# Attention scores and softmax of two 128-token blocks handled as one piece

## The chip, the cores and the metric

The kernel runs on one core of a Trainium2 chip. The metric is the device time of one launch in microseconds (us). Five engines work side by side and meet through semaphores: TensorE (PE in the profile, with its weight loads as PEld), VectorE (DVE), ScalarE (ACT), GpSimd (POOL) and SyncE (SP, which here only issues DMAs).

## What is computed

One transformer layer over x of 32 x 256 tokens x 256 features, in fp32: cross-attention with 8 heads to a context of 77 tokens, then a feed-forward network (FFN) with ternary weights, each behind a layer norm and with a residual.

```python
q = _heads(x @ Wq.T + bq)                 # x: layer norm of the input
k = _heads(y @ Wk.T + bk)                 # y: the 77 context tokens
v = _heads(y @ Wv.T + bv)
logits = einsum('bhqd,bhkd->bhqk', q, k) * scale + causal
attn = softmax(logits, axis=-1)
out = einsum('bhqk,bhkd->bhqd', attn, v) ... @ Wo.T + bo
# FFN: D_IN 256, D_HID 1024
h = silu(_tlin(x, w1_w, w1_s)) * _tlin(x, w2_w, w2_s)
h = gelu(_tlin(h, h1_w, h1_s)); h = gelu(_tlin(h, h2_w, h2_s))
return _tlin(h, w3_w, w3_s)
```

The causal mask is laid over 256 queries and 77 keys, so of a sequence's two blocks of 128 queries only the first has masked scores.

## The kernel before

The 8192 tokens are cut into 16 tiles of 512 tokens: two sequences (NB = 2), or four blocks of 128 tokens (NQ = 4, TQ // P = 2 of each sequence). The program is a software pipeline of passes. A first pass (the list FIRST, for `f is None`) does the attention of tile 0 while the weights arrive, are rounded (ROUND, on ACT) and compared (CHECK, on DVE). Then 15 passes do the FFN of tile f and the attention of tile f + 1 together, and a 16th does only the FFN of the last tile. 14 of the 15 are turns of a loop, the other two passes are written out behind it.

What stands next to what is an order written out by hand: the list ORDER of pairs (step, n). Every engine runs through the same list and issues, at each entry, whatever that step has for it; between engines there are only semaphores. So an entry's place in ORDER is its place in each engine's queue, and an instruction that waits holds up all that stands behind it on its engine.

The steps that matter here:

- L1 0 to 7 (FFN, first layer): PE 8 matmuls of 512 columns in two products (gate and up), ACT Silu of the gate (L492) and the rounding `a_hi` of the entry before (L501), DVE the product with up (L602) and the remainder `a_lo` of the entry before (L607). L1E does the last remainder. The `a_lo` feed L2.
- L2 0 to 7: PE 16 matmuls each; ACT two Gelu activations (L506, L507, the second signals `gelu2_done`); DVE the remainder `b_lo` (L613). L2 0 waits for `h1_done` before each of its k.
- S 0 to 3, one for each block of 128 tokens: 8 small matmuls (L434, each two instructions in the trace, so 16) write the scores of 8 heads to columns 0 to 153 of the four banks `att_banks`. Blocks 0 and 2 are masked straight from the banks by DVE (L637, signals `masked`), blocks 1 and 3 copied by ACT (L526, signals `s_copied`); since all four blocks use the same columns, PE waits for the read of the one before. DVE then takes the maximum per head (L641) and subtracts it (L643, signals `shifted`).
- EXP 0 to 3: ACT the exponential (L530, waits `shifted`), DVE in `soften` the sum (L578, waits `exp_done`), its reciprocal (L580) and the scaling (L582, signals `probs_ready`).
- PT 0 to 3: PE 8 transposes of the probabilities (L445), copied out half by ACT (L535) and half by DVE (L650, signals `pt_dve_done`). PV 0 and 1 (L454) multiply with v for one sequence and wait until both copies of both its blocks are done.

ACT holds one table of functions at a time. Silu, Gelu and Exp are in different ones, and the compiler puts an ACT_TABLE_LOAD ahead of the first activation that needs another.

Of the kernel before, what the change touches and what calls it, by code (L numbers as in the profile page):

```python
# [19 lines left out]
ALU = mybir.AluOpType  # L20
ACT = mybir.ActivationFunctionType
AX_X = mybir.AxisListType.X

P = 128
B, TQ, TK, D = 32, 256, 77, 256
H = 8
HD = D // H
HID = 1024
TILE = 512
NB = TILE // TQ  # L30
NT = B // NB
NQ = TILE // P
KD = D // P
KH = HID // P
HG = H // 4
G2 = 2 * TK


def column_of(head):
# [3 lines left out]
SCALE = float(HD) ** -0.5  # L43
# [6 lines left out]

ORDER = [
    ("L1", 0), ("T1", 0), ("L1", 1), ("KV", 0), ("L1", 2), ("Q", 0), ("L1", 3), ("S", 0),
    ("L1", 4), ("L1", 5), ("S", 1), ("L1", 6), ("S", 2), ("L1", 7), ("L1E", 0), ("S", 3),
    ("EXP", 0), ("EXP", 1), ("EXP", 2), ("EXP", 3),
# [10 lines left out]
def steps(ffn, att, nxt):  # L65
# [5 lines left out]

FIRST = [
    ("KV", 0), ("T1", 0), ("ROUND", 0), ("ROUND", 1), ("Q", 0), ("CHECK", 0), ("CHECK", 1), ("ROUND", 2),
    ("S", 0), ("S", 1), ("S", 2), ("ROUND", 3), ("S", 3), ("CHECK", 2), ("EXP", 0), ("EXP", 1), ("ROUND", 4), ("EXP", 2),
    ("EXP", 3), ("PT", 0), ("CHECK", 3), ("PT", 1), ("ROUND", 5), ("CHECK", 4), ("PV", 0),
    ("PT", 2), ("ROUND", 6), ("CHECK", 5), ("PT", 3), ("CHECK", 6), ("PV", 1), ("ROUND", 7), ("CHECK", 7), ("O", 0),
    ("ROUND", 8), ("CHECK", 8), ("ROUND", 9), ("CHECK", 9), ("ROUND", 10), ("CHECK", 10), ("COUNT", 0),
    ("LN2S", 0), ("LN2A", 0), ("T2", 0), ("LN1S", 0), ("LN1A", 0), ("CTX", 0),
]
# [2 lines left out]
def build_kernel(nc, x, ctx_t, w_att, vectors, w1, w2, h1, h2, w3, out):  # L82
# [4 lines left out]
    with ExitStack() as es:  # L87
# [36 lines left out]
        q_t, _ = put("q_t", [P, HG, TILE], at=b_lo_at + 4096)  # L124
# [16 lines left out]
        k_t, _ = put("k_t", [P, HG, NB * TK])  # L141
# [3 lines left out]
        probs, probs_at = put("probs", [P, NQ, H * TK])  # L145
# [4 lines left out]
        mask, _ = put("mask", [P, TK])  # L150
# [5 lines left out]
        mx, _ = put("mx", [P, NQ, H])  # L156
        total, _ = put("total", [P, NQ, H])
        rtotal, _ = put("rtotal", [P, NQ, H])
# [14 lines left out]
        ab = es.enter_context(nc.psum_tensor("att_banks", [P, 4, 512], F32))  # L173
# [22 lines left out]
        masked, s_ready, max_done, shifted, exp_done = sem("masked"), sem("s_ready"), sem("max_done"), sem("shifted"), sem("exp_done")  # L196
        s_copied = sem("s_copied")
        sum_done, rsum_done, probs_ready = sem("sum_done"), sem("rsum_done"), sem("probs_ready")
        pt_ready, pt_act_done, pt_dve_done = sem("pt_ready"), sem("pt_act_done"), sem("pt_dve_done")
        pv_ready, heads_done, o_ready = sem("pv_ready"), sem("heads_done"), sem("o_ready")  # L200
        x_biased, x1_done, x1_kept = sem("x_biased"), sem("x1_done"), sem("x1_kept")
# [30 lines left out]
        at = 0  # L232
# [68 lines left out]
        def _(pe):  # L301
# [37 lines left out]
            def one_pass(f, a, nxt, general):  # L339
                for step, n in steps(True, a is not None, nxt) if f is not None else FIRST:  # L340
# [35 lines left out]
                    if step == "L4":  # L376
# [3 lines left out]
                        for i in range(2):  # L380
                            j = 2 * n + i
# [6 lines left out]
                            else:  # L388
                                mm = product(fb[:, 2 + n, i * D:(i + 1) * D], lambda k: w3_sb[:, k, :], KH, hi, lo,
                                             wait_h, KH * f, w_is_moving=True)  # L390
# [4 lines left out]
                    if step == "T1":  # L395
                        pe.wait_ge(ln_ready[0], a + 1)
                        for k in range(KD):
                            for j in range(NQ):
                                mm = nc.tensor.transpose(ab[:, k, j * P:(j + 1) * P], xln[:, j, k * P:(k + 1) * P], id32[:])  # L399
# [13 lines left out]
                    if step == "Q":  # L413
                        pe.wait_ge(ln1t_done, a + 1)
                        for m in range(HG):
                            for k in range(KD):
                                mm = nc.tensor.matmul(ab[:, m, :], wq_sb[:, k, m * P:(m + 1) * P], ln1_t[:, k, :],  # L417
                                                      start=(k == 0), stop=(k == KD - 1))
                        mm.then_inc(q_ready, 1)
                    if step == "S":  # L420
                        if n == 0:
                            pe.wait_ge(q_done, a + 1)
                            pe.wait_ge(k_done, a + 1)
                            pe.wait_ge(v_done, a + 1)
                        if n == 1 or n == 3:
                            pe.wait_ge(masked, NB * a + n // 2 + 1)
                        if n == 2:
                            pe.wait_ge(s_copied, NB * a + 1)
                        keys = (n // (TQ // P)) * TK
                        for g in range(HG):  # L430
                            at = g * TK
                            for h in range(4):
                                rows = slice(HD * h, HD * (h + 1))
                                mm = nc.tensor.matmul(ab[:, h, at:at + TK], q_t[rows, g, n * P:(n + 1) * P],  # L434
                                                      k_t[rows, g, keys:keys + TK], start=True, stop=True)
                        mm.then_inc(s_ready, 1)
                    if step == "PT":
                        pe.wait_ge(probs_ready, NQ * a + n + 1)
                        if n < 2:
                            pe.wait_ge(shifted, NQ * a + NQ)  # L440
                        if n == 3:
                            pe.wait_ge(heads_done, NB * a + 1)
                        pair = (2, 0, 0, 2)[n]
                        for h in range(H):
                            mm = nc.tensor.transpose(ab[0:TK, pair + h // 4, (h % 4) * P:(h % 4 + 1) * P],  # L445
                                                     probs[:, n, column_of(h) * TK:(column_of(h) + 1) * TK], id32[:])
                        mm.then_inc(pt_ready, 1)
# [36 lines left out]
        def _(act):  # L484
            def one_pass(f, a, nxt):
                for step, n in steps(True, a is not None, nxt) if f is not None else FIRST:
# [30 lines left out]
                    if step == "Q":  # L517
# [1 line left out]
                        for g in range(HG):  # L519
                            op = nc.scalar.activation(q_t[:, g, :], ab[:, g, :], ACT.Identity, bias=bq_sb[:, g:g + 1])  # L520
                        op.then_inc(q_done, 1)
                    if step == "S" and n % (TQ // P) == 1:
                        act.wait_ge(s_ready, NQ * a + n + 1)
                        if n == 3 and not (isinstance(a, int) and a == 0):
                            act.wait_ge(x1_kept, a)
                        nc.scalar.copy(probs[:, n, :].rearrange("p (h g c) -> p h g c", g=HG, h=4),  # L526
                                       ab[:, :, 0:G2].rearrange("p h (g c) -> p h g c", g=HG)).then_inc(s_copied, 1)
                    if step == "EXP":
                        act.wait_ge(shifted, NQ * a + n + 1)
                        nc.scalar.activation(probs[:, n, :], probs[:, n, :], ACT.Exp, scale=SCALE).then_inc(exp_done, 1)  # L530
                    if step == "PT":
                        act.wait_ge(pt_ready, NQ * a + n + 1)
                        q0 = (n % 2) * P
# [21 lines left out]
        def _(dve):  # L555
# [15 lines left out]
                                                 ALU.subtract, ALU.mult)  # L571
                op.then_inc(ln_ready[i], 1)

            def soften(n, a):

                p = probs[:, n, :].rearrange("p (h c) -> p h c", h=H)
                dve.wait_ge(exp_done, NQ * a + n + 1)
                nc.vector.tensor_reduce(total[:, n, :], p, AX_X, ALU.add).then_inc(sum_done, 1)  # L578
                dve.wait_ge(sum_done, NQ * a + n + 1)
                nc.vector.reciprocal(rtotal[:, n, :], total[:, n, :]).then_inc(rsum_done, 1)  # L580
                dve.wait_ge(rsum_done, NQ * a + n + 1)
                nc.vector.tensor_tensor(p, p, rtotal[:, n, :].unsqueeze(2).broadcast_to([P, H, TK]), ALU.mult)\  # L582
                    .then_inc(probs_ready, 1)

            def one_pass(f, a, nxt):
                for step, n in steps(True, a is not None, nxt) if f is not None else FIRST:
# [34 lines left out]
                    if step == "KV":  # L621
                        dve.wait_ge(v_ready, a + 1)
                        nc.vector.tensor_tensor(v_sb[:], ab[0:TK, 3, :].rearrange("p (b d) -> p b d", b=NB),
                                                bv_sb[0:TK].unsqueeze(1).broadcast_to([TK, NB, D]), ALU.add).then_inc(v_done, 1)
                    if step == "S":
                        scores = ab[:, :, 0:G2].rearrange("p h (g c) -> p h g c", g=HG)
                        if n % (TQ // P) == 0:
                            dve.wait_ge(s_ready, NQ * a + n + 1)
                        else:
                            dve.wait_ge(s_copied, NB * a + n // 2 + 1)  # L630
                        m = mx[:, n, :].rearrange("p (h g) -> p h g", g=HG)
                        p = probs[:, n, :].rearrange("p (h g c) -> p h g c", g=HG, h=4)
                        if n == 2 and not (isinstance(a, int) and a == 0):
                            dve.wait_ge(x1_kept, a)
                        if n % (TQ // P) == 0:

                            nc.vector.tensor_tensor(p, scores, mask[:].unsqueeze(1).unsqueeze(1).broadcast_to([P, 4, HG, TK]),  # L637
                                                    ALU.add).then_inc(masked, 1)
                            dve.wait_ge(masked, NB * a + n // 2 + 1)
                        scores = p  # L640
                        nc.vector.tensor_reduce(m, scores, AX_X, ALU.max).then_inc(max_done, 1)  # L641
                        dve.wait_ge(max_done, NQ * a + n + 1)
                        nc.vector.tensor_tensor(p, scores, m.unsqueeze(3).broadcast_to([P, 4, HG, TK]), ALU.subtract)\  # L643
                            .then_inc(shifted, 1)
                    if step == "EXP":
                        soften(n, a)
                    if step == "PT" and f is not None:
                        dve.wait_ge(pt_ready, NQ * a + n + 1)
                        q0 = (n % 2) * P
# [122 lines left out]
```

## Time and profile before

| | us |
|---|---|
| median of 3 runs | 1685.14 (1684.5 to 1686.07) |
| the profiled execution | 1688.33 |
| its span in the trace | 1686.5 |
| one pass (two stretches of 101.30 and 101.45) | about 101.4 |

The span is what the trace shows from first to last instruction; the execution's own time is 1.8 us more. Start times in the rows are us from the span's start. A timeline row is: start, duration, engine, line, operation, output and inputs, count, and in brackets the idle time of the engine ahead of it and what ended it. Matmuls overlap, so for PE the distance between two starts counts and not the duration.

### The profile page before, as it was taken

How to read it: one execution, taken by the hardware profiler on the slowest of the kernel's cores; microseconds unless marked ns; L12 is line 12 of the kernel's file. 1: busy time of each engine (PE TensorE's matmuls, PEld its weight loads, DVE VectorE, ACT ScalarE, POOL GpSimd, SP SyncE). 2: the span in 40 equal slices, each digit the busy share in tenths (PEclk: the TensorE clock that was granted, in tenths of full speed). 3: DMA queues.
4: the chain of work that ended last, by engine and by line, in shares of the span. 5: the costliest groups of instructions: out<-in, count | busy, mean ns of one | idle time of the engine just before them, and what ended most of it. 6: DMA issues, size and time to landing. Idle time of an engine off the chain costs nothing.

```text
span 1686.5 us, 22398 instructions
## 1 busy us (share of the span) xinstructions
PE 1636.5 (97%) x9090; PEld 1324.1 (79%) x9090; DVE 818.4 (49%) x1449; ACT 742.9 (44%) x1136; POOL 119.1 (7%) x120
## 2 busy tenths in 40 slices
PE   4599999999999999999999999999999999999998
PEld 3478888787887878888787887878888787887887
DVE  6663634637255463634637255462644636345331
ACT  5453543535344353543535345353443535345342
POOL 1100101001010100101001010100101001010000
PEclk7699999999999999999999999999999999999999
DMA  7100000000000000000000000000000000000000
GB/s 300 42 1 13 16 12 16 0 16 12 12 16 0 21 7 12 16 9 19 0 16 12 12 16 0 16 12 12 16 1 27 0 16 12 12 17 1 1 13 13
DMA packets 21094, 32.60 MB, mean 19 GB/s; under 512 B 976, under 2 KB 19408, under 8 KB 19536
## 3 DMA queue, kind: packets, MB, share of 16 engines
q1 hardware_dynamic: 21072, 32.30, 5.6%
q8 instruction: 15, 0.25, 0.1%
q14 instruction: 7, 0.06, 0.0%
HBM read 23.91 MB, written 8.39 MB: 19 GB/s over the span
## 4 chain that ended last, share of the span: by engine, by line
PE 86%; DVE 8%; issue 3%; ACT 2%; DMA 0%; POOL 0%; DVEq 0%; SPq 0%; POOLq 0%; ACTq 0%
PE ffn_banks L309 68%; PE att_banks L445 4%; PE att_banks L462 3%; PE att_banks L417 3%; PE att_banks L454 2%; DVE a_lo L607 2%; DVE a_f L602 2%; PE att_banks L410 2%; DVE mx L641 2%; DVE probs L637 1%; PE att_banks L405 1%; PE att_banks L399 1%; PE att_banks L336 1%; DVE stage L595 1%; PE att_banks L434 1%
## 5 line engine op out<-in xcount | busy, mean ns | idle before, releaser
L309 PE MATMUL ffn_banks<-a_hi,h_sb 128*128 128x512 f32 x1024 | 408.6, 399 | 0.0
L309 PE MATMUL ffn_banks<-b_hi,h_sb 128*128 128x512 f32 x1024 | 401.3, 392 | 0.0
L309 PE MATMUL ffn_banks<-a_lo,h_sb 128*128 128x512 f32 x1024 | 400.2, 391 | 0.0
L309 PE MATMUL ffn_banks<-b_lo,h_sb 128*128 128x512 f32 x1024 | 398.6, 389 | 0.0
L506 ACT ACTIVATE a_f<-ffn_banks,vec 128x512 f32<-128x512 f32 x128 | 88.2, 689 | 354.2 <-PE ffn_banks L309 354.2
L613 DVE TENSOR_TENSOR a_lo<-a_f,a_hi 128x512 fp32r<-128x512 f32 x128 | 88.6, 692 | 317.8 <-ACT a_hi L507 317.8
L309 PEld LDWEIGHTS ffn_banks<-a_hi,h_sb 128*128 128x128 f32 x1024 | 192.3, 188 | 46.0 <-issue 6.2
L613 DVE TENSOR_TENSOR b_lo<-b_f,b_hi 128x512 fp32r<-128x512 f32 x128 | 85.8, 690 | 286.1 <-ACT b_hi L507 286.1
L309 PEld LDWEIGHTS ffn_banks<-b_hi,h_sb 128*128 128x128 f32 x1024 | 192.3, 188 | 39.8
L309 PEld LDWEIGHTS ffn_banks<-b_lo,h_sb 128*128 128x128 f32 x1024 | 192.3, 188 | 39.7
L309 PEld LDWEIGHTS ffn_banks<-a_lo,h_sb 128*128 128x128 f32 x1024 | 192.5, 188 | 38.4
L309 PE MATMUL ffn_banks<-ln_hi,w_sb 128*128 128x512 f32 x512 | 217.5, 425 | 2.4 <-DVE ln_lo L667 2.4
L309 PE MATMUL ffn_banks<-ln_lo,w_sb 128*128 128x512 f32 x512 | 202.5, 396 | 0.0
L506 ACT ACTIVATE b_f<-ffn_banks,vec 128x512 f32<-128x512 f32 x128 | 88.0, 688 | 249.2 <-PE ffn_banks L309 249.0
L492 ACT ACTIVATE a_f<-ffn_banks,vec 128x512 f32<-128x512 f32 x128 | 88.2, 689 | 178.3 <-PE ffn_banks L309 178.3
L602 DVE SCALAR_TENSOR_TENSOR a_f<-ffn_banks,vec,a_f 128x512 f32<-128x512 f32 x128 | 95.7, 748 | 145.4 <-ACT a_f L492 104.1
L309 PE MATMUL ffn_banks<-w_sb,a_hi 128*128 128x256 f32 x512 | 124.9, 286 | 0.4 <-DVE a_lo L613 0.4
L309 PE MATMUL ffn_banks<-w_sb,a_lo 128*128 128x256 f32 x512 | 123.5, 283 | 0.0
L309 PEld LDWEIGHTS ffn_banks<-ln_hi,w_sb 128*128 128x128 f32 x512 | 97.1, 190 | 28.6 <-issue 3.6
L309 PEld LDWEIGHTS ffn_banks<-ln_lo,w_sb 128*128 128x128 f32 x512 | 97.3, 190 | 21.8 <-issue 3.6
L692 POOL TENSOR_TENSOR veps<-mv,eps 128x4 f32<-128x4 f32 x32 | 6.4, 201 | 1336.6 <-DVE mv L564 1336.6
L309 PEld LDWEIGHTS ffn_banks<-w_sb,a_hi 128*128 128x128 f32 x512 | 98.2, 192 | 0.7 <-DVE a_lo L613 0.6
(81 smaller groups left out, 1942.6 us busy)
## 6 DMA issues: line engine op xcount, KB each, us to landing
x_in<-in_x SPq DMA_DIRECT2D x16, 512.0 KB, 3.8
stage<-in_h SPq DMA_DIRECT2D x8, 1024.0 KB, 14.2
out<-out_sb SPq DMA_DIRECT2D x16, 512.0 KB, 2.9
stage<-in_w SPq DMA_DIRECT2D x3, 1024.0 KB, 9.2
ctx_sb<-in_ctx_t SPq DMA_DIRECT2D x16, 154.0 KB, 2.2
w_att_sb<-in_w_att SPq DMA_DIRECT2D x1, 1024.0 KB, 7.2
vec<-in_vectors SPq DMA_DIRECT2D x1, 402.0 KB, 4.5
```

The costliest lines, as they stand in the source:

```text
L309: mm = nc.tensor.matmul(psum, left, right, start=(k == 0 and part == 0), stop=(k == rows - 1 and part == 1))
L410: mm = nc.tensor.matmul(ab[0:TK, 3, b * D:(b + 1) * D], ctx_sb[:, k, b * TK:(b + 1) * TK], wv_sb[:, k, :], start=(k == 0), stop=(k == KD - 1))
L417: mm = nc.tensor.matmul(ab[:, m, :], wq_sb[:, k, m * P:(m + 1) * P], ln1_t[:, k, :], start=(k == 0), stop=(k == KD - 1))
L445: mm = nc.tensor.transpose(ab[0:TK, pair + h // 4, (h % 4) * P:(h % 4 + 1) * P], probs[:, n, column_of(h) * TK:(column_of(h) + 1) * TK], i ...
L454: mm = nc.tensor.matmul(ab[HD * h:HD * (h + 1), bank, g * TQ:(g + 1) * TQ], v_sb[:, n, (4 * g + h) * HD:(4 * g + h + 1) * HD], attn_t[:, 4 ...
L462: mm = nc.tensor.matmul(ab[:, 2 + j // 2, (j % 2) * D:(j % 2 + 1) * D], heads_t[:, k, j * P:(j + 1) * P], wo_sb[:, k, :], start=(k == 0), ...
L492: nc.scalar.activation(a_f32[:, n, :], fb[:, 2 * (n % 2), :], ACT.Silu, scale=s1_sb[:, n:n + 1]).then_inc(silu_done, 1)
L506: nc.scalar.activation(f32[:, n, :], fb[:, n % 4, :], ACT.Gelu, scale=scale[:, n:n + 1])
L602: nc.vector.scalar_tensor_tensor(out=a_f32[:, n, :], in0=fb[:, 2 * (n % 2) + 1, :], scalar=s2_sb[:, n:n + 1], in1=a_f32[:, n, :], op0=ALU. ...
L607: nc.vector.tensor_tensor(a_lo[:, m, :], a_f32[:, m, :], a_hi[:, m, :].bitcast(F32), ALU.subtract)\
L613: nc.vector.tensor_tensor(lo[:, n, :], f32[:, n, :], hi[:, n, :].bitcast(F32), ALU.subtract).then_inc(done, 1)
L641: nc.vector.tensor_reduce(m, scores, AX_X, ALU.max).then_inc(max_done, 1)
```

## The change

S now has two entries, one for each sequence. Each issues 16 matmuls: those of the first block to columns 0 to 153 of each bank, those of the second to columns 154 to 307. ACT copies both blocks (1232 elements per partition) to `probs`, and DVE works from there only. What DVE did under S and EXP is split into steps of their own: MASK n (first block only, 616 elements), MAX n and SUB n and SOFT n (both blocks, 1232 elements, 16 sums). EXP n is one activation over 1232 elements. PT 0 waits for `probs_ready` of sequence 0 and for `s_copied` of sequence 1, PT 2 for `probs_ready` of sequence 1. In ORDER, SOFT 0 stands ahead of L2 0, MAX 1 and SUB 1 behind it, EXP 1 behind L2 1, and SOFT 1 between PT 0 and L2 3. FIRST is changed in the same manner.

```diff
 ORDER = [
     ("L1", 0), ("T1", 0), ("L1", 1), ("KV", 0), ("L1", 2), ("Q", 0), ("L1", 3), ("S", 0),
-    ("L1", 4), ("L1", 5), ("S", 1), ("L1", 6), ("S", 2), ("L1", 7), ("L1E", 0), ("S", 3),
-    ("EXP", 0), ("EXP", 1), ("EXP", 2), ("EXP", 3),
-    ("L2", 0), ("L2", 1), ("L2", 2), ("PT", 0), ("L2", 3), ("PT", 1), ("L2", 4), ("PV", 0),
+    ("L1", 4), ("MASK", 0), ("L1", 5), ("MAX", 0), ("S", 1), ("L1", 6), ("SUB", 0), ("L1", 7), ("L1E", 0),
+    ("EXP", 0), ("MASK", 1), ("SOFT", 0), ("L2", 0), ("MAX", 1), ("SUB", 1), ("L2", 1), ("EXP", 1),
+    ("L2", 2), ("PT", 0), ("SOFT", 1), ("L2", 3), ("PT", 1), ("L2", 4), ("PV", 0),
...
-                        if n == 1 or n == 3:
-                            pe.wait_ge(masked, NB * a + n // 2 + 1)
-                        if n == 2:
+                        else:
                             pe.wait_ge(s_copied, NB * a + 1)
...
+                        for half in range(2):
+                            tokens = slice((2 * n + half) * P, (2 * n + half + 1) * P)
+                            for g in range(HG):
+                                at = half * G2 + g * TK
+                                for h in range(4):
+                                    rows = slice(HD * h, HD * (h + 1))
+                                    mm = nc.tensor.matmul(ab[:, h, at:at + TK], q_t[rows, g, tokens],
+                                                          k_t[rows, g, n * TK:(n + 1) * TK], start=True, stop=True)
                         mm.then_inc(s_ready, 1)
                     if step == "PT":
-                        pe.wait_ge(probs_ready, NQ * a + n + 1)
-                        if n < 2:
-                            pe.wait_ge(shifted, NQ * a + NQ)
+                        if n % 2 == 0:
+                            pe.wait_ge(probs_ready, NB * a + n // 2 + 1)
+                        if n == 0:
+                            pe.wait_ge(s_copied, NB * a + NB)
...
-                        act.wait_ge(shifted, NQ * a + n + 1)
-                        nc.scalar.activation(probs[:, n, :], probs[:, n, :], ACT.Exp, scale=SCALE).then_inc(exp_done, 1)
+                        act.wait_ge(shifted, NB * a + n + 1)
+                        nc.scalar.activation(probs[:, 2 * n:2 * n + 2, :], probs[:, 2 * n:2 * n + 2, :],
+                                             ACT.Exp, scale=SCALE).then_inc(exp_done, 1)
...
+                    if step == "MASK":
+                        dve.wait_ge(s_copied, NB * a + n + 1)
...
+                    if step == "MAX":
+                        dve.wait_ge(masked, NB * a + n + 1)
+                        nc.vector.tensor_reduce(per_head(mx, n), heads_of(n), AX_X, ALU.max).then_inc(max_done, 1)
+                    if step == "SUB":
+                        dve.wait_ge(max_done, NB * a + n + 1)
+                        nc.vector.tensor_tensor(heads_of(n), heads_of(n), over_keys(mx, n), ALU.subtract).then_inc(shifted, 1)
+                    if step == "SOFT":
+                        dve.wait_ge(exp_done, NB * a + n + 1)
+                        nc.vector.tensor_reduce(per_head(total, n), heads_of(n), AX_X, ALU.add).then_inc(sum_done, 1)
+                        dve.wait_ge(sum_done, NB * a + n + 1)
+                        nc.vector.reciprocal(per_head(rtotal, n), per_head(total, n)).then_inc(rsum_done, 1)
+                        dve.wait_ge(rsum_done, NB * a + n + 1)
+                        nc.vector.tensor_tensor(heads_of(n), heads_of(n), over_keys(rtotal, n), ALU.mult).then_inc(probs_ready, 1)
```

ACT's queue from the last remainder's rounding of L1 on (`a_hi`), before; `b_f` and `b_hi` are the two Gelu of an L2 entry, `attn_t` the copy of PT 0:

```order
L501 CAST a_hi<-a_f_58 128x512 x2
L523 REGISTER_ALU
L526 COPY probs<-att_banks 128x616
L529 REGISTER_ALU
L530 ACT_TABLE_LOAD
L530 ACTIVATE probs<-probs 128x616 x2
L529 REGISTER_ALU
L530 ACTIVATE probs<-probs 128x616 x2
L506 ACT_TABLE_LOAD
L506 ACTIVATE b_f_59<-ffn_banks,vec 128x512
L507 ACTIVATE b_hi<-ffn_banks,vec 128x512
```

And now:

```order
L502 CAST a_hi<-a_f_58 128x512 x2
L531 ACT_TABLE_LOAD
L531 ACTIVATE probs<-probs 128x1232
L507 ACT_TABLE_LOAD
L507 ACTIVATE b_f_59<-ffn_banks,vec 128x512
L508 ACTIVATE b_hi<-ffn_banks,vec 128x512
L507 ACTIVATE b_f_59<-ffn_banks,vec 128x512
L508 ACTIVATE b_hi<-ffn_banks,vec 128x512
L531 ACT_TABLE_LOAD
L531 ACTIVATE probs<-probs 128x1232
L507 ACT_TABLE_LOAD
L507 ACTIVATE b_f_59<-ffn_banks,vec 128x512
```

The four exponentials stood together, between one pair of table loads. Now there are two, with the Gelu of L2 0 and L2 1 between them, and a pair of table loads for each.

DVE's queue from L2's first remainder (`b_lo`) to the copy of PT 1 (`attn_t`), before:

```order
L582 TENSOR_TENSOR probs<-probs,rtotal 128x616
L613 TENSOR_TENSOR b_lo<-b_f_59,b_hi 128x512 x3
L650 COPY attn_t<-att_banks 77x4x128
L613 TENSOR_TENSOR b_lo<-b_f_59,b_hi 128x512
L650 COPY attn_t<-att_banks 77x4x128
```

And now:

```order
L645 TENSOR_TENSOR probs<-probs,rtotal 128x1232
L616 TENSOR_TENSOR b_lo<-b_f_59,b_hi 128x512
L635 TENSOR_REDUCE mx<-probs 128x16
L638 TENSOR_TENSOR probs<-probs,mx 128x1232
L616 TENSOR_TENSOR b_lo<-b_f_59,b_hi 128x512 x2
L647 ISA
L649 COPY attn_t<-att_banks 77x4x128
L641 TENSOR_REDUCE total<-probs 128x16
L643 RECIPROCAL rtotal<-total 128x16
L645 TENSOR_TENSOR probs<-probs,rtotal 128x1232
L616 TENSOR_TENSOR b_lo<-b_f_59,b_hi 128x512
L647 REGISTER_ALU
```

Maximum and subtraction of sequence 1 moved behind the first `b_lo`, and its sum, reciprocal and scaling stand between the copy of PT 0 and that of PT 1, which is the next row.

## Rows read from the trace of the kernel before

**Rows 1.** The page: busy time, share of the span, instructions of PE

```profile
PE 1636.5 (97%) x9090; PEld 1324.1 (79%) x9090; DVE 818.4 (49%) x1449; ACT 742.9 (44%) x1136; POOL 119.1 (7%) x120
```

**Rows 2.** Busy time of each engine in one pass; the 1.00 is PEclk

```profile
184.30:285.75 101.45, 101.35 (x571) 82.09 (x570) 49.80 (x89) 45.00 (x71) 7.38 (x7) 1.00 0.04 12
```

**Rows 3.** Timeline of PE in that pass, from S 0 to PV 0

```profile
194.13 0.68 PE L434 MATMUL att_banks<-k_t,q_t 32*128 32x77 f32 x16
194.74 0.50 PE L309 MATMUL ffn_banks<-ln_hi,w_sb 128*128 128x512 f32 x1
...
199.25 0.50 PE L309 MATMUL ffn_banks<-ln_hi,w_sb 128*128 128x512 f32 x1
...
201.93 0.50 PE L309 MATMUL ffn_banks<-ln_hi,w_sb 128*128 128x512 f32 x1
...
224.96 1.07 PE L454 MATMUL att_banks<-attn_t,v_sb 77*32 77x256 f32 x16
```

**Rows 4.** The same timeline cut off at 194.20: only S 0's first instructions

```profile
194.13 0.35 PE L434 MATMUL att_banks<-k_t,q_t 32*128 32x77 f32 x4
```

**Rows 5.** Timeline of PE's weight loads: those of S 0 and of S 3

```profile
194.12 0.54 PEld L434 LDWEIGHTS att_banks<-k_t,q_t 32*128 32x128 f32 x16 [0.36 <-issue]
...
204.15 0.54 PEld L434 LDWEIGHTS att_banks<-k_t,q_t 32*128 32x128 f32 x16 [0.53 <-DVE probs L637]
```

**Rows 6.** Timeline of DVE, L1 6 to L1 7

```profile
202.04 0.74 DVE L602 SCALAR_TENSOR_TENSOR a_f<-ffn_banks,vec,a_f 128x512 f32<-128x512 f32 x1
202.70 0.68 DVE L607 TENSOR_TENSOR a_lo<-a_f,a_hi 128x512 fp32r<-128x512 f32 x1
203.30 0.79 DVE L637 TENSOR_TENSOR probs<-att_banks,mask 128x616 f32<-128x616 f32 x1
...
204.96 0.80 DVE L643 TENSOR_TENSOR probs<-probs,mx 128x616 f32<-128x616 f32 x1
205.68 0.74 DVE L602 SCALAR_TENSOR_TENSOR a_f<-ffn_banks,vec,a_f 128x512 f32<-128x512 f32 x1
```

**Rows 7.** Timeline of DVE, softmax of block 0, and the copy of PT 0

```profile
209.71 0.80 DVE L578 TENSOR_REDUCE total<-probs 128x8 f32<-128x616 f32 x1 [0.37 <-ACT probs L530]
210.54 0.20 DVE L580 RECIPROCAL rtotal<-total 128x8 f32<-128x8 f32 x1
210.78 0.80 DVE L582 TENSOR_TENSOR probs<-probs,rtotal 128x616 f32<-128x616 f32 x1
...
218.63 0.68 DVE L650 COPY attn_t<-att_banks 77x512 f32<-77x512 f32 x1
```

**Rows 8.** Timeline of ACT, from the last `a_hi` to the first Gelu

```profile
206.45 0.62 ACT L501 CAST a_hi<-a_f 128x512 fp32r<-128x512 f32 x1 [2.10 <-DVE a_f L602]
...
208.96 2.55 ACT L530 ACTIVATE probs<-probs 128x616 f32<-128x616 f32 x4
211.52 1.28 ACT L506 ACT_TABLE_LOAD   x1
212.82 0.69 ACT L506 ACTIVATE b_f<-ffn_banks,vec 128x512 f32<-128x512 f32 x1
213.40 0.68 ACT L507 ACTIVATE b_hi<-ffn_banks,vec 128x512 fp32r<-128x512 f32 x1
```

**Rows 9.** Groups of instructions: line, engine, form, count, busy us, mean ns

```profile
L530 ACT ACTIVATE probs<-probs 128x616 f32<-128x616 f32 x64 | 40.8, 707 | 0.2
L510 ACT COPY ln_t<-att_banks 128x1024 f32<-128x1024 f32 x16 | 16.1, 1004 | 5.5 <-PE att_banks L399 5.5
L658 DVE TENSOR_TENSOR x<-att_banks,x_in 128x1024 f32<-128x1024 f32 x16 | 19.6, 1225 | 23.4 <-PE att_banks L462 23.4
```

**Rows 10.** Timeline of ACT at the pass's start: Silu's table and its first user

```profile
173.43 1.28 ACT L492 ACT_TABLE_LOAD   x1
180.72 0.69 ACT L492 ACTIVATE a_f<-ffn_banks,vec 128x512 f32<-128x512 f32 x1 [6.01 <-PE ffn_banks L309]
```

**Rows 11.** Timeline of PE in the first pass: PV 0

```profile
40.29 1.93 PE L454 MATMUL att_banks<-attn_t,v_sb 77*32 77x256 f32 x16 [1.25 <-ACT attn_t L538]
```

More of the change, by code:

```diff
@@ L73 @@
     ("KV", 0), ("T1", 0), ("ROUND", 0), ("ROUND", 1), ("Q", 0), ("CHECK", 0), ("CHECK", 1), ("ROUND", 2),
-    ("S", 0), ("S", 1), ("S", 2), ("ROUND", 3), ("S", 3), ("CHECK", 2), ("EXP", 0), ("EXP", 1), ("ROUND", 4), ("EXP", 2),
-    ("EXP", 3), ("PT", 0), ("CHECK", 3), ("PT", 1), ("ROUND", 5), ("CHECK", 4), ("PV", 0),
-    ("PT", 2), ("ROUND", 6), ("CHECK", 5), ("PT", 3), ("CHECK", 6), ("PV", 1), ("ROUND", 7), ("CHECK", 7), ("O", 0),
+    ("S", 0), ("MASK", 0), ("MAX", 0), ("S", 1), ("SUB", 0), ("EXP", 0), ("MASK", 1), ("MAX", 1), ("SOFT", 0),
+    ("SUB", 1), ("ROUND", 3), ("EXP", 1), ("PT", 0), ("CHECK", 2), ("ROUND", 4), ("PT", 1), ("SOFT", 1),
+    ("CHECK", 3), ("ROUND", 5), ("PV", 0), ("PT", 2), ("CHECK", 4), ("ROUND", 6), ("PT", 3), ("CHECK", 5), ("PV", 1),
+    ("CHECK", 6), ("ROUND", 7), ("CHECK", 7), ("O", 0),
     ("ROUND", 8), ("CHECK", 8), ("ROUND", 9), ("CHECK", 9), ("ROUND", 10), ("CHECK", 10), ("COUNT", 0),
@@ L424, in one_pass @@
                             pe.wait_ge(v_done, a + 1)
-                        if n == 1 or n == 3:
-                            pe.wait_ge(masked, NB * a + n // 2 + 1)
-                        if n == 2:
+                        else:
                             pe.wait_ge(s_copied, NB * a + 1)
[L429 to L435, printed above, removed]
+                        for half in range(2):
[6 more added lines that the diff above has]
+                                                          k_t[rows, g, n * TK:(n + 1) * TK], start=True, stop=True)
                         mm.then_inc(s_ready, 1)
                     if step == "PT":
-                        pe.wait_ge(probs_ready, NQ * a + n + 1)
-                        if n < 2:
-                            pe.wait_ge(shifted, NQ * a + NQ)
+                        if n % 2 == 0:
+                            pe.wait_ge(probs_ready, NB * a + n // 2 + 1)
+                        if n == 0:
+                            pe.wait_ge(s_copied, NB * a + NB)
                         if n == 3:
@@ L521, in one_pass @@
                         op.then_inc(q_done, 1)
-                    if step == "S" and n % (TQ // P) == 1:
-                        act.wait_ge(s_ready, NQ * a + n + 1)
-                        if n == 3 and not (isinstance(a, int) and a == 0):
+                    if step == "S":
+                        act.wait_ge(s_ready, NB * a + n + 1)
+                        if n == 1 and not (isinstance(a, int) and a == 0):
                             act.wait_ge(x1_kept, a)
-                        nc.scalar.copy(probs[:, n, :].rearrange("p (h g c) -> p h g c", g=HG, h=4),
-                                       ab[:, :, 0:G2].rearrange("p h (g c) -> p h g c", g=HG)).then_inc(s_copied, 1)
+                        nc.scalar.copy(probs[:, 2 * n:2 * n + 2, :].rearrange("p j (h x) -> p j h x", h=4),
+                                       ab[:, :, 0:2 * G2].rearrange("p h (j x) -> p j h x", j=2)).then_inc(s_copied, 1)
                     if step == "EXP":
-                        act.wait_ge(shifted, NQ * a + n + 1)
-                        nc.scalar.activation(probs[:, n, :], probs[:, n, :], ACT.Exp, scale=SCALE).then_inc(exp_done, 1)
+                        act.wait_ge(shifted, NB * a + n + 1)
+                        nc.scalar.activation(probs[:, 2 * n:2 * n + 2, :], probs[:, 2 * n:2 * n + 2, :],
+                                             ACT.Exp, scale=SCALE).then_inc(exp_done, 1)
                     if step == "PT":
@@ L572, in ln_apply, with heads_of, per_head, over_keys @@
                 op.then_inc(ln_ready[i], 1)
[L574 to L583, printed above, removed]
+            def heads_of(n):
+                return probs[:, 2 * n:2 * n + 2, :].rearrange("p j (h c) -> p (j h) c", h=H)
+            def per_head(t, n):
+                return t[:, 2 * n:2 * n + 2, :].rearrange("p j h -> p (j h)")
+            def over_keys(t, n):
+                return per_head(t, n).unsqueeze(2).broadcast_to([P, 2 * H, TK])
             def one_pass(f, a, nxt):
@@ L624, in one_pass @@
                                                 bv_sb[0:TK].unsqueeze(1).broadcast_to([TK, NB, D]), ALU.add).then_inc(v_done, 1)
[L625 to L644, printed above, removed]
@@ L645, in one_pass @@
-                    if step == "EXP":
-                        soften(n, a)
+                    if step == "MASK":
+                        dve.wait_ge(s_copied, NB * a + n + 1)
+                        scores = probs[:, 2 * n, :].rearrange("p (h c) -> p h c", h=H)
+                        nc.vector.tensor_tensor(scores, scores, mask[:].unsqueeze(1).broadcast_to([P, H, TK]), ALU.add)\
+                            .then_inc(masked, 1)
+                    if step == "MAX":
+                        dve.wait_ge(masked, NB * a + n + 1)
+                        nc.vector.tensor_reduce(per_head(mx, n), heads_of(n), AX_X, ALU.max).then_inc(max_done, 1)
```

## The prediction, made before the changed kernel ran

> **What bounds the kernel now.** I read the busy times first: PE works 97% of the span, DVE 49%, ACT 44% [rows 1]. The busy times of one pass sharpen that: in 101.45 us PE is busy for 101.35, at a granted clock of 1.00, its upper level of 2.4 GHz [rows 2]. In a steady pass PE is the bound and practically never waits, so a pass gets shorter only where PE has less to do, and longer as soon as it waits. 15 passes have the changed steps; the FFN-only pass has none of them. Then the timeline of PE, for what the S slots cost it, and those of DVE and ACT, for the chain of softmax, which so far ran well ahead of its user.
>
> **PE's side: what the merged slots save.** From L1 4's first matmul (194.74) to L1 6's (199.25) lie two L1 blocks and one S slot, 4.51 us; from there to L1 7's (201.93) one block and one slot, 2.68 [rows 3]. The difference, 1.83, is a block, so a slot costs 0.85. Of S 0's 16 instructions the first four span 0.35 [rows 4] and all 16 span 0.68 [rows 3]: 0.11 for each four more. A slot of 32 then costs 0.85 + 4 x 0.11 = 1.29, 0.41 less than two slots; a pass saves 0.82. Also, S 3's weight loads begin 0.53 after the ones before and S 0's 0.36 [rows 5]: 0.17 of waiting for the mask of block 2. That wait goes: S 1 waits only for ACT's copy of S 0, which is over almost 3 us earlier. If nothing else held PE, a pass would be 0.99 shorter and the kernel 15 us faster.
>
> **What is late next: a chain to PV 0.** PV 0 needs DVE's copy of PT 1, and this copy now stands behind SOFT 1. SOFT 1 needs EXP 1, which needs SUB 1, which stands behind SOFT 0, which needs EXP 0. I walk this from L1 6's first matmul, taken as 0, on steps measured between starts. A DVE operation of 1232 instead of 616 elements: 1024 take 1.225 [rows 9] and 616 take 0.80 [rows 6], 1.04 ns per element, so 0.64 more. A reduction of 616 lets its user start after 0.83 [rows 7], so 1.47 now; a subtraction or scaling lets an independent one start after 0.72 [rows 6], so 1.36 now, and lasts 1.44. The Exp of 616 takes 0.707 [rows 9] and four back to back 2.55 [rows 8], so the second half adds no more than 0.61; by ACT's copy of 1024 in 1.004 [rows 9] it adds 0.45. I take the middle, 0.53, so 1.24.
>
> - L1 6's up product is ready at about 2.17 (seven distances of 0.23, some 0.15 of restart behind the slot, the last matmul's 0.4). Product to remainder 0.66, remainder to SUB 0 0.60 [rows 6], SUB 0 to L1 7's product 1.36, from there to the last `a_hi` on ACT 0.77 [rows 6, 8]: 5.56.
> - `a_hi` 0.62, table load and start 1.31, EXP 0 1.24, to DVE 0.05 [rows 8, 9]: 8.78.
> - SOFT 0: sum 1.47, reciprocal 0.24 [rows 7], scaling 1.36; `b_lo` of L2 0 0.60, MAX 1 1.47, SUB 1 1.44: 15.36. The Gelu of L2 0, 1.26 long behind its own load, ends near 11.3 and doesn't hold DVE.
> - EXP 1 0.04 and 1.24, the Gelu table 1.31, the first Gelu of L2 2 0.58, the second 0.68 [rows 8]: 19.21.
> - To DVE 0.04; `b_lo` of L2 2 0.60; copy of PT 0 0.60; SOFT 1 3.07; `b_lo` of L2 3 0.60; copy of PT 1 0.68 [rows 6, 7]; PE starts 0.10 later: 24.90.
>
> PE itself would come to PV 0 at 224.96 - 199.25 = 25.71 [rows 3], less S 2 and S 3 and the wait: 25.71 - 1.70 - 0.17 = 23.84. So PE waits for 1.06 there, some of it already in L2 0: the last `a_lo` of L1 ends at about 6.9 where PE would like it near 6.8. These two are one wait, since the chain doesn't start from L2. The second Exp load has room: ACT is through with L2 1's Gelu at about 12.8 and SUB 1 ends at 15.36, and a load doesn't wait for its user's semaphore. Silu's load ran at 173.43, its user only at 180.72, idle for the 6.01 between [rows 10]. The Gelu load behind EXP 1 is in the chain and counted.
>
> **The sum.** S 0 to L1 6 was 5.12 and is 5.12 + 2 x 0.44 = 6.00. To PV 0: 6.00 + 24.90 = 30.90 against 224.96 - 194.13 = 30.83 before. The gain on PE is given back nearly whole: +0.07 a pass, +1.1 over 15. Behind PV 0 all is as before; PT 2 needs SOFT 1's scaling, which ends over 1 us ahead. In the first pass PV 0 waits for ACT's copies, at 40.29 [rows 11]; the same steps walked with its order (ACT's rounding between, PT 1 ahead of SOFT 1) put it at about 39.95, so -0.3. Against the execution's own 1688.33 that is 1689.1. The execution was 3.2 above the median of the runs; I carry this over: **1685.9**.
>
> **Bounds.** Small matmuls: the trace has no run of 32. Below, the 0.44 for 16 more; above, a second slot's whole 0.85, +0.41 a slot. I take 0.44, as the same operation at its own pace. Exp: 0.08 either way, twice a pass. DVE's seven long operations: 0.03 each either way, since 1024 elements in other forms are the nearest row. The starts behind a semaphore: 0.04 to 0.15. Together about 0.25 a pass, 4 us, and up to 12 us above from the slots.
>
> **Two rules weighed.** Between the end of the last Exp (211.51) and the load, and between the load's end and the Gelu, lie 0.01 and 0.02 [rows 8]. The Trainium skill (ScalarE: Activation LUTs, What ACT_TABLE_LOAD costs) has each switch cost a drain of some 1380 ns beside the 1283 ns of the load, which would speak against splitting the exponentials; by it the two loads in the chain would add 2.7 us a pass, some 41 us in all, an estimate. The trace has the load alone.
>
> **The rivals.** (1) The long S slot doesn't keep its pace. PE may issue 16 small matmuls out of its queue quickly and the next 16 slowly; if these cost as much as a slot's start to next product, 0.61 [rows 3], a pass is 0.17 x 2 = 0.34 longer, 1691; at 0.85 each 0.82 longer, 1698. It decides from 0.07 a slot on, since the chain starts behind both. For it: no such run in the trace. Against: in S 0 the last twelve go at the pace of the first. The Trainium skill (TensorE: Matmul & The Clock Gate, Wait — 56ns, not 53.3ns?) has a sequencer that spends about 62 ns per matmul with hardware decoding off; at that pace for the second 16 a slot would take 0.55 more, an estimate, and the kernel about 1702. (2) The wait at PV 0 stays small: DVE's long operations and the Exp are at their short ends and the chain loses 0.3 to 0.5 a pass. 1679 to 1682; if it didn't reach PV 0 at all, 1671. For it: each step is an upper reading where forms differ. Against: the sum exceeds PE's own arrival by 1.06, five times its likely error. (3) A table switch holds the activation longer than the load, or the second Exp load waits for SUB 1: 1.3 more in the chain for one of them, 1705, twice that for both. Against it stand [rows 8, 10].
>
> **Chances.** Forecast, gain and wait within 0.2 a pass of each other: 0.58. Rival 1, with the share of the forecast's spread above it: 0.22. Rival 2 likewise below: 0.16. Rival 3: 0.04. A measurement here tells about 0.2%, 3.4 us, from no change. So faster 0.16, same 0.58, slower 0.26. The range holds 8 in 10: from 1680.5, inside rival 2, to 1693.5, inside rival 1.
>
> **What would show it.** In the changed trace: S slots of 32 instructions spanning about 1.12; no wait ahead of S 1; an Exp load that starts soon after L2 1's Gelu and well ahead of EXP 1; DVE's copy of PT 1 ending just as PV 0 starts, with PE's wait of about 1 us ahead of it, on `attn_t`. The distance S 0 to PV 0 near 30.9. I am wrong if PV 0 starts right behind L2 4 (faster), if a slot spans over 1.4, or if ACT idles behind a load.

## The result and the profile after

The changed kernel takes 1692.4 us (median of 6 runs, 1691.11 to 1693.0) against 1685.43 for the kernel before (6 runs): a ratio of 1.0034 with an interval of 1.0024 to 1.0044. It is slower, by 7.0 us (4.0 to 7.4 by the interval). Two executions, one of the kernel before (2418.98 us) and one of a later variant (4951.11 us), ran far slower than all others and are left out of every comparison. The forecast was 1685.9 with a range to 1693.5, so the time lies in the range's upper part and on the side to which I gave 0.26.

One pass in the new trace, the same columns as in [rows 2] (length, busy time of PE, PEld, DVE, ACT and POOL with their instructions, granted clock, share and GB/s of the DMAs):

```profile
195.28:296.93 101.65, 100.72 (x569) 82.05 (x568) 48.52 (x79) 48.52 (x72) 7.38 (x7) 1.00 0.04 12
```

PE now leaves 0.93 of a pass idle where it left 0.10. Measured from the first pass's S 0 to the fifteenth's (93.64 to 1516.82, 14 distances), a pass takes 101.656; before it took 101.463 (92.65 to 1513.13). That is +0.193 a pass and 2.9 us in all. PE's waits, all of them over the whole span (first the total, then how often, then the longest):

```profile
PE att_banks L455 <- DVE attn_t L649: 14.3, 15, 1.0
...
PE att_banks L337 <- issue: 2.1, 1, 2.1
```

The first is the forecast wait: 15 times ahead of PV 0, for DVE's copy of PT 1, 0.95 each. The second I had not forecast. The timeline of PE, answering [rows 3]:

```profile
195.28 1.13 PE L434 MATMUL att_banks<-k_t,q_t 32*128 32x77 f32 x32
...
200.24 1.13 PE L434 MATMUL att_banks<-k_t,q_t 32*128 32x77 f32 x32
201.30 0.50 PE L310 MATMUL ffn_banks<-ln_hi,w_sb 128*128 128x512 f32 x1
...
226.31 1.07 PE L455 MATMUL att_banks<-attn_t,v_sb 77*32 77x256 f32 x16 [0.93 <-DVE attn_t L649]
```

S 0 to L1 6 takes 6.02 (forecast 6.00), L1 6 to PV 0 25.01 (24.90), together 31.03 (30.90). And the chain that ended last, for the same stretch, which can be laid beside the steps of the prediction one by one (start, duration, what):

```profile
206.87 0.62 ACT a_hi L502
207.49 0.02 issue
207.51 1.28 ACT L531
208.79 0.01 issue
208.81 1.24 ACT probs L531
210.05 0.02 issue
210.07 1.45 DVE total L641
...
215.25 1.45 DVE probs L638
216.71 0.02 issue
216.73 0.05 ACT probs L531
216.78 1.20 issue
217.98 1.28 ACT L507
...
225.57 0.61 DVE attn_t L649
226.18 0.14 issue
226.31 0.38 PE att_banks L455
```

A table load, EXP 0, SOFT 0, then MAX 1 and SUB 1 (`probs` L638), EXP 1, the Gelu load, the Gelu, and the copy of PT 1 at the end. ACT around the second exponential:

```profile
214.01 1.28 ACT L531 ACT_TABLE_LOAD   x1
216.73 1.23 ACT L531 ACTIVATE probs<-probs 128x1232 f32<-128x1232 f32 x1 [1.43 <-DVE probs L638]
217.98 1.28 ACT L507 ACT_TABLE_LOAD   x1
219.27 0.69 ACT L507 ACTIVATE b_f<-ffn_banks,vec 128x512 f32<-128x512 f32 x1
```

The Exp load is over 1.43 before SUB 1 lets EXP 1 start: it is hidden. The Gelu load behind EXP 1 is not.

### The profile page after: what moved, and what is told of

Read it like the earlier page. It is cut to its first block, busy times and chain, and to the rows that moved or that the text cites. A ratio compares the mean times of both kernels' runs of the same rounds, so it can differ in the third digit from the quotient of the medians.

```text
span 1690.4 us, 22161 instructions
## 1 busy us (share of the span) xinstructions
PE 1625.6 (96%) x9090; PEld 1323.1 (78%) x9090; DVE 797.7 (47%) x1289; ACT 796.4 (47%) x1134; POOL 119.1 (7%) x120
## 4 chain that ended last, share of the span: by engine, by line
PE 76%; DVE 13%; ACT 6%; issue 4%; DMA 0%; POOL 0%; SPq 0%; POOLq 0%; ACTq 0%; DVEq 0%
PE ffn_banks L310 59%; PE att_banks L463 3%; PE att_banks L418 3%; DVE total L641 3%; PE att_banks L455 2%; PE att_banks L434 2%; PE att_banks L446 2%; DVE probs L638 2%; PE att_banks L411 2%; DVE probs L645 1%; DVE mx L635 1%; ACT probs L531 1%; DVE b_lo L616 1%; ACT L507 1%; ACT L531 1%
```

## The experiments

My theory after the result: inside the passes the merged slots save 0.8 to 1 us a pass, and the chain over two separate exponentials gives back more than that; ahead of the loop something else costs some 4 us, part of it the stall of 2.1.

**Both kernels once more.** No edit.

> The changed kernel once more, unaltered, for a second profile. First theory (the chain to PV 0): S slots of 32 spanning 1.13 us, PE's wait of 0.9 to 1.0 ahead of every PV 0, a pass of 101.66, 6 to 7 us above the kernel before. Second theory (a good part of the 7 us is a single stall of 2.06 us in PE's transposes between the first pass and the loop, where the profile names no releaser): that stall is there again at the same place, since it would belong to this program's code. If it was chance, it is gone and the span is some 2 us shorter.

> The kernel before once more, unaltered, for a second profile and for the scatter of the comparison. Ratio 1.000 within 0.001. The profiled execution of before was 3 us above its median; if a stall outside the passes is to blame, this profile has a span near 1683.5 with passes of 101.46 as in the first, and the 3 us are missing ahead of the loop.

Measured: the changed kernel 1693.05, ratio 1.0040 (1.0027 to 1.0054); the kernel before 1685.95 against 1685.28, ratio 1.0003 (0.9994 to 1.0012). The passes repeat to the hundredth: 101.657 and 101.464. The stall is there again, at the same instruction; first the changed kernel once more, then the kernel before once more, transposes ahead of the loop:

```profile
68.25 0.90 PE L337 MATMUL att_banks<-id,xln 128*128 128x128 f32 x3 [4.76 <-DVE xln L572]
71.15 1.33 PE L337 MATMUL att_banks<-id,xln 128*128 128x128 f32 x5 [2.00 <-issue]
```

```profile
67.86 1.97 PE L336 MATMUL att_banks<-id,xln 128*128 128x128 f32 x8 [4.77 <-DVE xln L570]
```

The second profile of before has a span of 1683.4, 3.1 shorter than the first, all of it ahead of the loop (its first S 0 of the passes starts at 89.47 instead of 92.65). So the comparison of the two first profiles, +3.9 us of span, understated the difference.

**All softmax ahead of L2.**

```diff
-    ("EXP", 0), ("MASK", 1), ("SOFT", 0), ("L2", 0), ("MAX", 1), ("SUB", 1), ("L2", 1), ("EXP", 1),
-    ("L2", 2), ("PT", 0), ("SOFT", 1), ("L2", 3), ...
+    ("EXP", 0), ("MASK", 1), ("MAX", 1), ("SUB", 1), ("EXP", 1), ("SOFT", 0), ("SOFT", 1), ("L2", 0), ("L2", 1),
+    ("L2", 2), ("PT", 0), ("L2", 3), ...
```

> The changed kernel with one edit to its order in the passes: MASK 1, MAX 1, SUB 1, EXP 1, SOFT 0 and SOFT 1 all ahead of L2 0. The merged slots stay; the two exponentials share one pair of table loads and SOFT 1 no longer stands between the two copies. First theory (the merged slots save 0.8 to 1.0 a pass and the chain to PV 0 gives it back): PE's wait ahead of PV 0 is gone, a pass takes 100.6 to 100.8, the kernel is 10 to 15 us faster than before. Rival (the long slots themselves, or a wait at L2 0, eat the gain): a pass stays at 101.3 or above and the kernel within 2 us of before.

Measured 1677.62, ratio 0.9954 (0.9940 to 0.9967): 7.7 us faster than before. A pass, and PE from L2 4 on:

```profile
195.00:295.60 100.60, 100.60 (x570) 82.04 (x569) 48.52 (x79) 45.66 (x70) 7.38 (x7) 1.00 0.04 12
```

```profile
224.67 0.39 PE L310 MATMUL ffn_banks<-a_lo,h_sb 128*128 128x512 f32 x1
224.98 1.07 PE L455 MATMUL att_banks<-attn_t,v_sb 77*32 77x256 f32 x16
```

No wait at PV 0: it starts 0.31 after the matmul ahead of it, in the kernel before 0.32. A pass takes 100.63, 0.83 less than before and 1.03 less than in the changed kernel. The merged slots gain most of the 0.99 they were costed at; what is missing is a small new wait in L2 0, told further on. 15 x 0.83 = 12.5 us should have shown, and 7.7 do. The rest, some 5 us, is lost ahead of the loop, where this kernel has the stall too: its first S 0 of the passes starts at 94.34, against 89.47 in the second profile of before.

**Only the exponentials together.** SOFT 1 stays between the copies.

```diff
-    ("EXP", 0), ("MASK", 1), ("SOFT", 0), ("L2", 0), ("MAX", 1), ("SUB", 1), ("L2", 1), ("EXP", 1),
+    ("EXP", 0), ("MASK", 1), ("MAX", 1), ("SUB", 1), ("EXP", 1), ("SOFT", 0), ("L2", 0), ("L2", 1),
     ("L2", 2), ("PT", 0), ("SOFT", 1), ("L2", 3), ("PT", 1), ...
```

> The changed kernel with MAX 1, SUB 1 and EXP 1 ahead of L2 0 (so one pair of table loads a pass instead of two), but SOFT 1 left where the change put it, between the copies of PT 0 and PT 1. Theory (the wait at PV 0 needs the whole chain over the second exponential and its Gelu load; SOFT 1's place alone is harmless): L2 2's Gelu no longer waits for EXP 1, the copy of PT 1 ends at least 1 us ahead of PV 0, a pass of 100.6, the same time as with all softmax ahead, 1677.6. Rival (SOFT 1 between the copies is what costs): a wait ahead of PV 0 stays, a pass above 101.

Measured 1676.84, ratio 0.9946 (0.9932 to 0.9959), a pass of 100.604, no wait at PV 0. DVE:

```profile
218.08 0.68 DVE L649 COPY attn_t<-att_banks 77x512 f32<-77x512 f32 x1
218.68 1.42 DVE L641 TENSOR_REDUCE total<-probs 128x16 f32<-128x1232 f32 x1
...
222.39 0.68 DVE L649 COPY attn_t<-att_banks 77x512 f32<-77x512 f32 x1
```

SOFT 1 still lies between the copies and takes as long, but the whole piece runs earlier: the copy of PT 1 ends at 223.07, PE's PV 0 starts at 224.67. SOFT 1's place alone costs nothing.

**Only SOFT 1 moved.**

```diff
-    ("L2", 2), ("PT", 0), ("SOFT", 1), ("L2", 3), ("PT", 1), ("L2", 4), ("PV", 0),
+    ("L2", 2), ("PT", 0), ("L2", 3), ("PT", 1), ("SOFT", 1), ("L2", 4), ("PV", 0),
```

> The changed kernel with SOFT 1 moved behind PT 1 (one place in the order of the passes), so that DVE's copy of PT 1 runs ahead of it. First theory: the wait ahead of PV 0 goes, but PT 2, right behind PV 0, now meets the end of SOFT 1: PE waits there about 0.5 us instead of 0.93, a pass of about 101.25. 4 to 7 us faster than the changed kernel, about the time of before. Rival (SOFT 1 was not what PV 0 waited for): nothing moves.

Measured 1682.37, ratio 0.9978 (0.9968 to 0.9988), about 10 us faster than the changed kernel and already faster than before; a pass of 100.983. I had expected a pass of about 101.25 and 4 to 7 us, so it gained more than forecast. The wait changed its place and got shorter (the view ends at 227, so the second row counts only the first of PT 2's matmuls):

```profile
225.48 1.07 PE L455 MATMUL att_banks<-attn_t,v_sb 77*32 77x256 f32 x16
226.88 0.33 PE L446 MATMUL att_banks<-id,probs 128*77 128x128 f32 x1 [0.33 <-DVE probs L645]
```

PV 0 comes on time and PT 2, the next step, waits for SOFT 1's scaling, 0.33 where I expected 0.5. So either of the two edits, alone, ends the wait at PV 0: it takes the late second exponential and SOFT 1 ahead of the copy together. Only keeping the exponentials together leaves no wait behind; moving SOFT 1 alone keeps 0.35 to 0.38 a pass.

**The chain longer by one operation.**

```diff
+                        if n == 1 and f is not None:
+                            nc.vector.tensor_reduce(mx[:, 0, :], probs[:, 3, :].rearrange("p (h c) -> p h c", h=H), AX_X, ALU.max)
                         nc.vector.tensor_reduce(per_head(total, n), heads_of(n), AX_X, ALU.add).then_inc(sum_done, 1)
```

> The changed kernel with one more DVE operation in SOFT 1, a maximum over 616 elements whose result nobody uses, 0.72 us in the chain. Theory (the chain alone sets PV 0): every PV 0 comes 0.72 later, a pass of 102.35 to 102.4, 10 to 11 us slower than the changed kernel. Rival (PE's wait comes from something beside DVE and has slack against it): less than half of that.

Measured 1702.87, ratio 1.0101 (1.0086 to 1.0116), 10 us above the changed kernel. S 0 to PV 0 went from 31.03 to 31.74, a pass to 102.357: of 0.72 put in, 0.70 came out. PE's waits at PV 0:

```profile
PE att_banks L455 <- DVE attn_t L651: 25.1, 15, 1.7
```

**The chain shorter by one operation.** In the passes the scaling of sequence 1 is left out; the reciprocal signals in its place.

```diff
+                        if n == 1 and f is not None:
+                            nc.vector.reciprocal(per_head(rtotal, n), per_head(total, n)).then_inc(probs_ready, 1)
+                        else:
...
+                            nc.vector.tensor_tensor(heads_of(n), heads_of(n), over_keys(rtotal, n), ALU.mult).then_inc(probs_ready, 1)
```

> The changed kernel without the scaling by the reciprocal for sequence 1 of each tile in the passes (its outputs are left unscaled, part of the computation is left out): 1.36 us less in the chain ahead of PV 0. Theory (max of the chain and PE's own arrival, the wait being 0.93 and some of the distance already lost at L2 0): the wait is gone and the rest of the 1.36 buys nothing: S 0 to PV 0 goes from 31.03 to 30.0, a pass of 100.6 to 100.7, 14 to 16 us below the changed kernel. Rival (time follows DVE's work one for one): 1.36 a pass, 20 us.

Measured 1677.69, ratio 0.9951 (0.9935 to 0.9968), a pass of 100.623, S 0 to PV 0 30.0. Of 1.36 taken out, 1.03 came back: down to PE's own arrival and no further. Together with the run before it this shows that the later of two paths sets PV 0, the chain or PE's own work, and that the chain was the later one by 1.03.

**PE's code moved by 16 instructions.** In the branch for weights that don't round exactly, which this input never takes:

```diff
             with pe.If(count > 0):
+                for _ in range(16):
+                    nc.tensor.drain()
                 transpose_ln2(0)
```

> The changed kernel with 16 drains added to PE's program in the branch for weights that don't round exactly, which this input never takes. Nothing that runs is changed; only the place in memory of PE's code behind that branch moves by 16 instructions. Theory of code loading (the 2.0 us stall inside the transposes of the branch that is taken is PE waiting for its next piece of code, whose border lies a few instructions into them): the stall is gone or lies elsewhere, loop entry comes 2 us or more earlier, the kernel is 2 to 4 us faster than the changed one; the passes stay at 101.66. Rival (the stall comes from the branch itself or from the merged first pass): it stays at the same instruction and the time too.

> The order with all softmax ahead of L2, with the same 16 drains in the branch not taken. By the theory of code loading 1673.5 to 1676, 2 to 4 us faster than that order without them, and about 10 us faster than before; by the rival the same time as without them, 1677.6.

Measured: the changed kernel so padded 1690.77, ratio 1.0029 (1.0017 to 1.0041), about 2 us below both series of it without padding (1692.4 and 1693.05), its passes at 101.663. The order with softmax ahead, padded, 1674.49 (median of five), ratio 0.9935 (0.9922 to 0.9948), 3 us below its unpadded form and the fastest of all: 11 us below before. Its five executions lie in two groups, 1671.42 and 1671.55 at a mean granted clock of 0.988 and 1674.49 to 1676.77 at 0.984 to 0.986; the unpadded form had 0.984 or 0.985 in all five, so part of its 3 us is the clock's. In both the transposes are whole again; in the padded changed kernel:

```profile
68.47 1.97 PE L337 MATMUL att_banks<-id,xln 128*128 128x128 f32 x8 [4.94 <-DVE xln L574]
```

All unpadded kernels with the merged slots (seven profiles) have the stall, 2.0 to 2.1 us in six of them and 2.4 in the one without the scaling, at the fourth traced matmul; neither of the two profiles of before and neither of the two of padded kernels has it. Nothing that ran was changed, so the place of the code decides. The profile names no releaser but "issue"; that PE waits there for its code to arrive is the likeliest reading, and no row shows the fetch itself. The intervals of the padded and the unpadded kernel overlap, so the 2 us rest on the traces first, on the times second. The distance from PE's last matmul ahead of the branch (L473, now L474) to the passes' first S 0 agrees, if profiles with the same clock are compared. Where the next 8 transposes (L399, now L400) take 1.09 or 1.10, it is 26.56 and 26.57 without the stall and 28.83 to 28.93 with it; where they take 1.97, at the lower clock, it is 28.20 and 28.78 without and 31.11 to 31.36 with it.

## Why the prediction came out as it did

**PE's side: right, but for a small wait.** A slot of 32 spans 1.13 (1.12 forecast) and the merged slots keep the pace of the short ones, so rival 1 falls: S 0 to L1 6 6.02 for 6.00. The wait for block 2's mask is gone and none came ahead of S 1. Without the chain a pass takes 100.60 to 100.63, 0.83 to 0.86 less than before; forecast was 0.99, "if nothing else held PE". Something else does, the last `a_lo` of L1, which the prediction put at about 6.9 where PE would like it near 6.8 and counted only as a part of the chain's wait. PE's weight loads wait for it once a pass in every kernel with the merged slots and in none of these 15 passes of the kernel before. In the order with all softmax ahead, that wait (total, times, longest) and PE's matmuls there:

```profile
PEld ffn_banks L310 <- DVE a_lo L610: 3.9, 15, 0.3
```

```profile
207.98 0.50 PE L310 MATMUL ffn_banks<-a_hi,h_sb 128*128 128x512 f32 x1
208.31 0.39 PE L310 MATMUL ffn_banks<-a_lo,h_sb 128*128 128x512 f32 x1
208.54 0.40 PE L310 MATMUL ffn_banks<-a_hi,h_sb 128*128 128x512 f32 x1
```

One distance is 0.33 instead of 0.23, so 0.10 of the missing 0.13 to 0.16 goes there, with the chain or without it. Of the rest 0.02 is the slots'.

**The chain to PV 0: right in mechanism and place, 0.11 short.** The forecast's table against the trace, in us from step to step: last `a_hi` to EXP 0's start 1.94 (1.93), EXP 0 to SOFT 0 1.26 (1.29), sum 1.47 (1.47), reciprocal to scaling 0.29 (0.24), scaling to `b_lo` 1.36 (1.36), MAX 1 to SUB 1 1.46 (1.47), SUB 1 to EXP 1 1.48 (1.48), copy of PT 1 to PV 0 0.82 (0.78). The reciprocal is in it twice; it now has 16 sums instead of 8, and I had carried the 8's 0.24 over. The DVE rate of 1.04 ns per element and the half-way value for the Exp held: 1.42 to 1.44 for 1232 elements on DVE, 1.23 for the Exp. Rival 3 falls with the two starts behind the loads, 0.01 to 0.02. The 1.06 by which the chain was to exceed PE's own arrival was four times the stated error of 0.25, not five; it came out at 1.03.

**The two paths' difference: mis-sized.** The forecast had +0.07 a pass and the trace has +0.193. 0.11 of the gap is the chain's and 0.02 the slots'. On a difference of two terms of 1 us each, 0.12 is small, but times 15 it is 1.8 us. Alone it would not have made the kernel slower by the prediction's own measure: the passes cost 2.9 us, and it took 3.4 to tell a change from none. The other 4.1 of the 7.0 lie ahead of the loop.

**Ahead of the loop: wrong.** The step "in the first pass PV 0 ... -0.3" was forecast as the only effect there. The start of that pass differs between profiles, so I count from its first S 0 to PV 0: 18.76 (from 21.53 to the 40.29 of [rows 11]) and 18.33 before, 18.36 and 18.37 in the changed kernel, 0.4 less or nothing. That term was of the right size. What failed is that nothing else was in the sum: it put the difference ahead of the loop at -0.3, and it came to about +4. The prediction had no term for the code: 2.0 to 2.1 us of stall, shown by the padding. It had none for the clock either. What stays of the 7.0 us between the medians is 7.0 - 2.9 - 2.1 = 2.0. The traces show time at the lower clock there. Granted clock and PE's work in two stretches behind the stall, first before once more, then the changed kernel once more:

```profile
70.00:80.00 10.00, 7.08 (x28) 5.43 (x29) 5.27 (x16) 5.90 (x7) 3.61 (x3) 0.67 0.00 0
80.00:95.00 15.00, 15.00 (x88) 10.46 (x87) 8.32 (x13) 7.00 (x13) 0.00 (x0) 1.00 0.00 1
```

```profile
70.00:80.00 10.00, 5.76 (x16) 4.06 (x17) 4.95 (x15) 3.92 (x4) 1.83 (x3) 0.50 0.00 0
80.00:95.00 15.00, 15.00 (x75) 10.93 (x77) 3.75 (x6) 6.38 (x11) 1.73 (x1) 0.86 0.00 1
```

PE is at its lower level of 1.2 GHz (0.50) for all of the first stretch and part of the second, where the kernel before was through with it earlier: the pass's first 8 transposes take 1.97 against 1.09. But the first profile of before shows 1.97 too, and the padded changed kernel as well, and the first profile of the changed kernel 1.10. So the clock's rise there falls differently from run to run.

On average the change does shift it. Of the kernel before's 48 executions with a clock on record, 26 have a mean granted clock of 0.988, with a median of 1685.02 us, and 22 have 0.985 or 0.986, with 1686.75. All 17 executions of the changed kernel, padded or not, have 0.984 to 0.986. Its 11 unpadded ones have a median of 1692.57: 5.8 above those 22, and the passes and the stall make 5.0 of that. So some 1.2 of the 2.0 goes with the clock, by estimate from these medians, and 0.8 stays open. Why the changed kernel never gets the higher value is open. The stall alone is not the reason, since the padded changed kernel has none and stays at 0.984 to 0.986.

So the range held the time partly by luck. It was wide for the S slots and for the steps of the chain, and these came out nearly as forecast; what filled it lies ahead of the loop, and no rival named it. The 0.26 for slower was given to rivals 1 and 3 and to the spread above the forecast, and neither rival came.

**The rules weighed.** That a switch of tables costs a drain of 1380 ns beside the load (the Trainium skill, ScalarE: Activation LUTs, What ACT_TABLE_LOAD costs) is not what this trace shows: 0.01 to 0.02 lie on either side of a load, with 30 loads more in the kernel than before. The load's own length is the page's (group of the new profile: count, busy us, mean ns):

```profile
L531 ACT ACT_TABLE_LOAD x30 | 38.5, 1283 | 0.5
```

By the 62 ns per matmul (the Trainium skill, TensorE: Matmul & The Clock Gate, Wait — 56ns, not 53.3ns?) a slot of 32 would have spanned near 1.7, an estimate; it spans 1.13.

## What to carry to other kernels

When the bound engine gets less to do, write down when its next user's data will be ready and when the engine now arrives: the gain is the distance between the two, and a reordering that splits a group (here four exponentials between one pair of table loads) can lengthen that chain by the table load, two waits and everything queued in between. Here merging with the exponentials kept together gives 8 to 9 us, and 11 in the padded variant, and the order around it took that back; the fix is to keep the exponentials together. A forecast near zero that is the difference of two larger terms deserves a wide range, and its sign rests on terms as small as a reciprocal's 0.05. And when one launch is compared with another, what lies outside the loop belongs in the sum: here it cost more than the 15 passes did.

## What the runs showed of the hardware

- Small matmuls of 32 rows and 77 columns keep 0.11 us per four over a run of 32 (span 0.68 for 16, 1.13 for 32, at a granted clock of 1.00).
- PE can stall 2.0 to 2.4 us, once, in the middle of a straight run of instructions behind a taken branch, and 16 unexecuted instructions ahead of the target removed it in both kernels where they were tried. It costs as much as 0.14 us in every one of 15 passes.
- A table load doesn't wait for its user's semaphore: one ran 2.72 us ahead of its user's start (214.01 and 216.73) while that user waited for a semaphore.
